# One fp32 transformer layer with eight routed experts on one core: scaled rows scattered back to token order, weights split during attention, and a plan made ahead of the experts

## What is computed

```python
mod = silu(c) @ wmod                      # six rows of 256 for each batch: sa, ca, ga, sb, cb, gb
h = layernorm(x) * (1 + ca) + sa
x = x + ga * attention(h)                 # one head of 128, keys of the whole batch
h = layernorm(x) * (1 + cb) + sb
shared = (silu(h @ sg) * (h @ su)) @ sd   # 256 -> 512 -> 256
scores, experts = top_k(sigmoid(h @ router + bias), 2);  scores /= sum(scores)
combined = sum over the two chosen e of scores[e] * (silu(h @ gate[e]) * (h @ up[e])) @ down[e]
out = x + gb * (shared + combined)
```

## Time and profile before

| | |
|---|---|
| time, median of 3 | 1787.32 us |
| the profiled execution: its own time, its span | 1788.52 us, 1786.8 us |
| PE busy | 1645.2 us (92%), 10888 instructions |
| DVE busy | 1046.3 us (59%) |
| ACT busy | 826.2 us (46%) |
| POOL busy | 497.9 us (28%) |
| moved by DMA | 134.34 MB, 75 GB/s over the span |

### The profile page before, as it was taken

One profiled execution on the slowest core, in us unless ns is written; L12 is line 12 of the kernel. 1 busy time (PEld: TensorE's weight loads), 2 busy tenths in 40 slices (PEclk: granted clock), 3 DMA queues, 4 the chain that ended last, 5 costly groups with the idle time before them and its releaser, 6 DMA issues. The chain is left out here.

```text
span 1786.8 us, 34539 instructions
## 1 busy us (share of the span) xinstructions
PE 1645.2 (92%) x10888; PEld 1492.6 (84%) x10889; DVE 1046.3 (59%) x2242; ACT 826.2 (46%) x1628; POOL 497.9 (28%) x504
## 2 busy tenths in 40 slices
PE   8899999999999959897609999999999999988997
PEld 7899999999999848797508888888888888877886
DVE  6777777777778757576533333333333333338987
ACT  5566666565655545455203333333333333335553
POOL 4423223222000030654751020111022400007775
PEclk9999999999999969999859999999999999999999
DMA  3211111111011060211252121122122111114544
GB/s 113 95 43 42 42 42 45 40 47 37 25 37 36 25 230 7 89 73 60 104 192 99 53 88 56 53 91 88 54 90 90 53 53 56 53 43 122 159 144 139
DMA packets 102463, 134.34 MB, mean 75 GB/s; under 512 B 11620, under 2 KB 89572, under 8 KB 102252
## 3 DMA queue, kind: packets, MB, share of 16 engines
q1 hardware_dynamic: 85948, 86.56, 14.8%
q0 software_dynamic: 15312, 44.58, 7.5%
q10 hardware_dynamic: 1120, 2.10, 0.3%
HBM read 79.71 MB, written 53.49 MB: 75 GB/s over the span
## 5 line engine op out<-in xcount | busy, mean ns | idle before, releaser
L794 DVE TENSOR_TENSOR e_aT_lo<-e_bank,e_aT_hi 128x512 fp32r<-128x512 f32 x136 | 94.1, 692 | 239.2 <-ACT e_aT_hi L781 239.2
L757 PE MATMUL e_bank<-e_w_hi,e_xT_hi 128*128 x544 | 225.9, 415 | 0.0
L757 PE MATMUL e_bank<-e_w_hi,e_xT_lo 128*128 x544 | 214.0, 393 | 0.0
L757 PE MATMUL e_bank<-e_w_lo,e_xT_hi 128*128 x544 | 213.3, 392 | 0.0
L800 DVE TENSOR_TENSOR e_prod<-e_silu_g,e_bank 128x512 f32<-128x512 f32 x136 | 93.6, 688 | 189.9 <-PE e_bank L757 189.9
L1394 ACT ACTIVATE e_y<-e_bank 128x256 f32<-128x256 f32 x136 | 52.2, 384 | 320.8 <-PE e_bank L33 320.8
L1565 POOL DMA_INDIRECT y<-y_rows,place_i x128 | 131.7, 1029 | 218.1 <-POOLq L1253 179.4
L608 DVE TENSOR_REDUCE bmax<-s_pair 128x1 f32<-128x512 f32 (+1 forms) x192 | 166.1, 866 | 12.1 <-PE s_pair L33 9.1
L346 ACT ACTIVATE pT_hi<-t_pair 128x512 fp32r<-128x512 f32 (+1 forms) x192 | 136.0, 749 | 78.6 <-PE t_pair L470 76.8
L627 DVE TENSOR_TENSOR pT_lo<-t_pair,pT_hi 128x512 fp32r<-128x512 f32 (+1 forms) x192 | 160.1, 862 | 17.5 <-ACT pT_hi L346 15.5
L339 ACT ACTIVATE prob<-s_pair,negmax 128x1024 f32<-128x1024 f32 x128 | 141.7, 1116 | 57.1 <-DVE negmax L620 51.2
(11 more groups left out here) (294 smaller groups left out, 4562.9 us busy)
## 6 DMA issues: line engine op xcount, KB each, us to landing
e_h<-x_rows SPq DMA_DIRECT2D x136, 128.0 KB, 2.0
y_rows<-e_y SPq DMA_DIRECT2D x136, 128.0 KB, 1.7
XS<-in_x SPq DMA_DIRECT2D x32, 256.0 KB, 2.7
XR<-in_x SPq DMA_DIRECT2D x32, 256.0 KB, 2.6
x<-XR SPq DMA_DIRECT2D x32, 256.0 KB, 2.1
out<-Z SPq DMA_DIRECT2D x16, 512.0 KB
Z<-x SPq DMA_DIRECT2D x2, 2048.0 KB, 15.6
e_w_raw<-in_gate_w POOLq DMA_DIRECT2D x7, 512.0 KB, 4.2
```

Of the source, the lines that this page charges most:

```text
L757: mm = pe.matmul(out[:, 0:I], l, w, start=(c == 0 and k == 0), stop=(c == HC - 1 and k == 2))
L794: dve.tensor_tensor(flat(aT_lo, par), a_bank[:, 0:I], flat(aT_hi, par).bitcast(F32), ALU.subtract).then_inc(f.aT_lo_done, 1)
```

## The change

- **Weights.** All 27 matrices (three shared, 24 of the experts) are split during attention: SP loads one in a row-block (`load_piece`), POOL splits it (`split_piece`), SP stores both parts to `w_parts` in DRAM (`store_piece`). Nothing is split afterwards. The shared parts are loaded once and stay (`w_shared`); each expert's six parts are one DMA of 3 MB from SP into one of two halves of `w_all`.
- **Statistics** of the new rows are joined during attention on DVE (`join_statistics`) and finished on POOL (`deviations`).
- **Shared stage.** DVE writes the normalised rows straight into a ring of four groups of four steps; ACT's copy is gone. There are eight groups. Each row in the ring and in `x_rows` is four numbers longer: token, first place, and two numbers from which either score follows. After the 32 double steps eight single steps follow with tiles 32 to 39; during these the counts are known, the pads are stored, and DVE makes the plan in three parts. All groups are sent before the stage ends.
- **Experts.** ACT issues the loads of rows. DVE copies the four numbers (`rides`) and makes destination and score (`tell`). ACT scales the output by the score, and POOL scatters it with one indirect DMA to the token's row of `y_rows`, first choices in one half and second in the other. SP only loads weights.
- **Last stage.** 24 steps. There are no gathers: SP loads chunks of four tiles from both halves of `y_rows`, six chunks ahead; POOL adds them and multiplies by the gate row; DVE adds them to `Z`.

```diff
+            def load_piece(i):
+                if i:
+                    sp.wait_ge(piece_out, 32 * i)
+                sp.dma_start(piece_raw[:], d.matrices[i]).then_inc(piece_in, 16)
+
+            def store_piece(i):
+                sp.wait_ge(piece_split, 2 * i + 2)
+                o = W * (i % 3)
+                for part, src in enumerate((piece_hi[:].bitcast(F32), piece_raw[:])):
+                    sp.dma_start(d.w_parts[i // 3, :, part, o:o + W], src).then_inc(piece_out, 16)
...
+                if 0 <= G - 2 < PIECES:
+                    store_piece(G - 2)
+                if 0 <= G - 1 < PIECES:
+                    load_piece(G - 1)
...
+            def split_piece(i):
+                pool.wait_ge(piece_in, 16 * i + 16)
+                pool.tensor_copy(piece_hi[:], piece_raw[:]).then_inc(piece_split, 1)
+                pool.wait_ge(piece_split, 2 * i + 1)
+                pool.tensor_tensor(piece_raw[:].bitcast(F32R), piece_raw[:], piece_hi[:].bitcast(F32),
+                                   ALU.subtract).then_inc(piece_split, 1)
...
+                if m >= NG + 2:
+                    split_piece(m - NG - 2)
+                for b in range(NB - 2):
+                    if m == NG * (b + 2) + 4:
+                        deviations(pool, d, b)
...
+                for b in range(NB - 1):
+                    if G == NG * (b + 1) + 2:
+                        dve.wait_ge(d.stats1_done, 2 * NG * (b + 1))
+                        join_statistics(dve, d, b)
...
+def join_statistics(dve, d, b):
...
+    tb = slice(d.TB * b, d.TB * b + d.TB)
+    mean = lambda k: d.stats1[:, tb, 3 * k + 1]
+    second = lambda k: d.stats1[:, tb, 3 * k + 2]
+    gap, both, squares = d.mean_gap[:, tb], d.mean_sum[:, tb], d.squares[:, tb]
+    dve.tensor_tensor(gap, mean(0), mean(1), ALU.subtract).then_inc(d.moments, 1)
+    dve.tensor_tensor(both, mean(0), mean(1), ALU.add).then_inc(d.moments, 1)
+    dve.tensor_tensor(squares, second(0), second(1), ALU.add).then_inc(d.moments, 1)
+    dve.wait_ge(d.moments, 5 * b + 3)
+    dve.scalar_tensor_tensor(out=gap, in0=gap, scalar=(d.row - 4) / 4.0, in1=gap,
+                             op0=ALU.mult, op1=ALU.mult).then_inc(d.moments, 1)
+    dve.wait_ge(d.moments, 5 * b + 4)
+    dve.tensor_tensor(squares, squares, gap, ALU.add).then_inc(d.moments, 1)
+
...
+def deviations(pool, d, b):
+
+    tb = slice(d.TB * b, d.TB * b + d.TB)
+    pool.wait_ge(d.moments, 5 * b + 5)
+    pool.tensor_scalar(d.mean_gap[:, tb], d.squares[:, tb], 1.0 / (d.row - 4), EPS, ALU.mult, ALU.add
+                       ).then_inc(d.rstd_done, 1)
+    pool.wait_ge(d.rstd_done, 2 * b + 1)
+    pool.tensor_tensor(d.rstd[:, tb], d.mean_gap[:, tb], d.minus_half[:], ALU.pow).then_inc(d.rstd_done, 1)
...
+def columns_of(parts, lo_at, o, n):
+
+    return lambda c: parts[:, o + n * c:o + n * c + n], lambda c: parts[:, lo_at + o + n * c:lo_at + o + n * c + n]
...
+        spare = d.w_all[:, 1, :].bitcast(F32)
+        SLOT = 2 * GS * ROW
+        in_slot = lambda ap: ap.rearrange("p (s t h) -> p s t h", s=2, t=GS)
+        h_rows = [in_slot(spare[:, SLOT * i:SLOT * i + SLOT]) for i in range(RING // 2)]
+        h_rows += [sb(f"h_rows{i}", [P, 2, GS, ROW], F32) for i in range(RING // 2)]
...
+            for k in range(3):
+                if k == 2:
+                    sp.dma_start(rows[:, :, 0:H], d.mod_d.rearrange("o (b n) -> o b n", b=NB)[:, :, 3 * H:4 * H]
+                                 .to_broadcast([P, NB, H])).then_inc(gate_loaded, 16)
+                for part in range(2):
+                    o = 3 * W * part + W * k
+                    sp.dma_start(d.w_shared[:, o:o + W].bitcast(F32), d.w_parts[0, :, part, W * k:W * k + W]
+                                 ).then_inc(w_loaded[2 + k], 16)
             for b in ORDER:
...
+            sp.wait_ge(d.s_const, d.n_tables)
+            sp.dma_start(d.x_rows[d.spare_row:d.spare_row + P * E, :].rearrange("(e p) h -> p e h", p=P),
+                         d.pad[:].unsqueeze(1).to_broadcast([P, E, ROW])).then_inc(padded, 16)
+            sp.dma_start(d.w_all[:, 0, :].bitcast(F32), d.w_parts[1].rearrange("p a n -> p (a n)")).then_inc(d.w_ready, 16)
+            sp.wait_ge(free_known, 1)
+            for e in range(E):
+                row = sp.value_load(free_i[0:1, e:e + 1], min_val=0, max_val=d.all_rows - P)
+                sp.dma_start(d.x_rows[ds(row, P), :], d.pad[:]).then_inc(padded, 16)
             for b in ORDER:
                 sp.wait_ge(x_loaded[b], 16)
+            sp.wait_ge(gate_loaded, 16)
+            sp.wait_ge(d.w_ready, 16)
...
-            def shift(m, par, b):
+            def shift(m):
                 dve.wait_ge(scaled_done, m + 1)
-                if inside(m - 2, STEPS):
-                    dve.wait_ge(f.xT_mm, m - 1)
-                    dve.wait_ge(copied, m - 1)
-                dve.tensor_tensor(h[:, par, :, :], scaled[:, par, :, :], both_halves(b, H),
+                g = m // GS
+                if m < STEPS and m % GS == 0 and g >= RING:
+                    dve.wait_ge(sent[g % RING], ONCE * (g // RING))
+                dve.tensor_tensor(rows_at(m), scaled[:, m % 2, 0:streams(m), :], both_halves(m, H),
                                   ALU.add).then_inc(f.rows_ready, 1)
...
+            def plan_ends():
+                dve.wait_ge(sent[PLAN_GROUP % RING], ONCE * (PLAN_GROUP // RING + 1))
+                op(dve.tensor_tensor(count[:], base[:, GROUPS, :], d.first_row[:, 0:E], ALU.subtract))
+                op(dve.tensor_tensor(over, count[:].unsqueeze(2).to_broadcast([P, E, d.most]),
+                                     c.limits[:].unsqueeze(1).to_broadcast([P, E, d.most]), ALU.is_gt))
+                op(dve.tensor_reduce(nblocks[:], over, AX_X, ALU.add))
+                op(dve.tensor_copy(ends[:], nblocks[:]))
+                for e in range(1, E):
+                    op(dve.tensor_tensor(ends[:, e:e + 1], ends[:, e - 1:e], nblocks[:, e:e + 1], ALU.add))
+
+            def plan_experts():
+                op(dve.memset(starts[:, 0:1], 0.0))
+                op(dve.tensor_copy(starts[:, 1:E + 1], ends[:]))
+                op(dve.scalar_tensor_tensor(out=moved[:], in0=starts[:], scalar=-float(P), in1=d.first_row[:, 0:E + 1],
+                                            op0=ALU.mult, op1=ALU.add))
+                op(dve.tensor_tensor(jump[:], moved[:, 1:E + 1], moved[:, 0:E], ALU.subtract))
+                op(dve.tensor_tensor(behind[:], c.numbers[:].unsqueeze(2).to_broadcast([P, NBLK, E]),
+                                     ends[:].unsqueeze(1).to_broadcast([P, NBLK, E]), ALU.is_ge))
+                op(dve.memset(expert_of[:, 0:2], 0.0))
+                op(dve.tensor_reduce(expert_of[:, 2:], behind[0:1, :, 0:E - 1], AX_X, ALU.add))
+                by_pair = expert_of[:].rearrange("o (i two) -> o i two", two=2)
+                digit = [by_pair[:, 0:NBLK // 2, 0], by_pair[:, 0:NBLK // 2, 1],
+                         by_pair[:, 1:NBLK // 2 + 1, 0], by_pair[:, 1:NBLK // 2 + 1, 1]]
+                so_far = digit[3]
+                for k in (2, 1, 0):
+                    op(dve.scalar_tensor_tensor(out=packed[:, k], in0=so_far, scalar=float(E), in1=digit[k],
+                                                op0=ALU.mult, op1=ALU.add))
+                    so_far = packed[:, k]
+                op(dve.tensor_copy(d.table[:, 1, 0:NBLK // 2], packed[:, 0]))
+
+            def plan_rows():
+                op(dve.tensor_tensor(behind[:], behind[:], jump[:].unsqueeze(1).to_broadcast([P, NBLK, E]), ALU.mult))
+                op(dve.tensor_reduce(moved_by[:], behind[:], AX_X, ALU.add))
+                op(dve.tensor_tensor(d.block_rows[:], c.own_rows[:], moved_by[:], ALU.add))
+                op(dve.tensor_copy(d.table[:, 0], d.block_rows[0:1]))
+                op(dve.tensor_copy(d.ends_i[:], ends[0:1]))
...
+                if n % GS == 0 and 0 < n <= STEPS:
+                    place(n // GS - 1)
+                if n % GS == GS - 1 and n < STEPS:
+                    choose(n // GS)
+                if n == STEPS:
+                    dve.tensor_copy(free_i[:], base[0:1, GROUPS, :]).then_inc(free_known, 1)
+                if n == STEPS + 2:
+                    plan_ends()
+                if n == STEPS + 3:
+                    plan_experts()
+                if n == STEPS + 4:
+                    plan_rows()
...
+            for e in range(1, E):
+                if e >= 2:
+
+                    end = sp.value_load(d.ends_i[0:1, e - 2:e - 1], min_val=1, max_val=NBLK)
+                    hold(sp, d, f.y_mm, end)
+                    sp.wait_ge(d.w_ready, 16 * e)
+                sp.dma_start(d.w_all[:, e % 2, :].bitcast(F32), d.w_parts[e + 1].rearrange("p a n -> p (a n)")
+                             ).then_inc(d.w_ready, 16)
+            sp.wait_ge(d.w_ready, 16 * E)
...
+            def scatter(m, par):
+                if inside(m - 1, NBLK):
```

(68 more changed lines are left out.)

910 lines of the change are left out of this document (361 added, 549 removed).

## The result

The changed kernel takes 1875.61 us (median of 4 runs, 1872.39 to 1877.09) against 1787.88 us for the kernel before beside it: 1.0487 of its time, 95% interval 1.0469 to 1.0505. It is slower by 88 us; 1775 was forecast. The profiled execution has a span of 1870.6 us, 83.8 more than before's 1786.8.

What follows compares the result with a forecast made beforehand. PE was taken to bound the experts at 4.84 us a block, POOL's gathers to pace the last stage. Terms -1 + 28 + 15 - 54 = -12 us from 1787.3 gave 1775 us, range 1738 to 1808.

Steps and rivals of the forecast that it cites:

- The loop: Experts: ride, ACT's load, output, low parts and product close a loop once a block, 5.05 us against 4.84; +28 us.
- Rival 2: Experts: the loop is 5.25 us or more, through register read and issue in ACT's queue; 1809 at 5.3; chance 0.16.
- Rival 4: Experts: the register read is slow on ACT, 0.454 us, so the loop is 5.23 us; 1799; chance 0.04.
- The weight loads: Experts: six weight loads of 7.7 us delay rows issued 8 us before their need, 2.5 us each; +15 us.
- rival 3: Loop 5.05 us, but each of six weight loads stalls the block 5 us and last-stage chunks come late; 1800; chance 0.10.
- The last stage: Steps of 4.68 us, POOL's sums running ahead and DVE's wide additions in idle time; 135.8 us in all, -53.7 us.
- Before the first shared product: Kernel start to first shared product: attention's additions +1 us, start of the shared stage gains 5 us; -4.
- The 31 double-step intervals: Shared stage: a ring of four groups removes 31.5 us of waits, seven group ends cost 28.7; -3 us.
- the single steps with the plan and the way into the experts: Last double step to first expert product: 51 us for eight single steps and plan, 25.3 into the experts; 76.3 us.
- 11.5 - 6 = 5.7: Single steps: the plan's 27 DVE operations take 11.5 us in three places, 2 us hidden in each; 5.7 left.
- POOL's 27 splits: Attention: loading, splitting and storing 27 pieces falls in POOL's idle time; put at 0, bounds 0 and +8 us.
- Rival 1: Experts: the loop does not bind, PE keeps 4.84 us a block, weight loads cost some 8 us; 1740; chance 0.28.

Runs made afterwards that it cites:

- weights_in_six: Changed kernel with each of the last six experts' 3 MB weight loads cut into six loads, one released a block; experts 710.7 us, 46.1 less; whole time 1906.0 us.
- all_four: Changed kernel with ride and score ahead of DVE's product, weight loads in six spaced pieces, POOL's last-stage operations 256 columns wide; 1738.73 us, 0.9711 of the kernel before.
- the first four kernels: Changed kernel with one edit each, sharing a chip: load later, ride earlier, weight loads cut, POOL operations shortened; 1900.1, 1864.1, 1906.0, 1922.3 us.

## Why the prediction was wrong

Three prices were wrong, all three too low; 1875.6 lies above the whole range (1738 to 1808) and above every rival.

**The loop: right in kind, mis-sized.** "Sum 5.05 us against 4.84" is 5.02 in the trace, and its terms (eight are listed, not ten) hold within 0.1 us each: the load, for one, is 1.24 instead of 1.32. But I compared only this loop with PE's pace, and that step failed: the same chain also closes over two blocks with a whole PE step in it, and that one takes 5.28 a block, 5.25 in the mean of the 129 blocks without a stall: +55 us (135 x 0.41) instead of +28. Two cyclic paths shared the slow piece, and I had summed only the shorter. Rival 2 (5.25 or more) was the case that came, by this cause and not by its own, the register read and the issue in ACT's queue. Rival 4 is out, since the read takes 0.284 us on ACT (the row is in the last section). The Trainium skill, "DMA: Bandwidth & Descriptors", section "Latency and other measured facts", has a floor of about 600 ns for it; this trace does not agree, and the measurement decides.

**The weight loads: +48 instead of +15.** "A load is issued 8 us before its transposed copy is needed" is the step that failed: it is 5 us (1042.08 to 1047.0, when PE was through with the products and had nothing but these rows to turn). The 8 is that of the kernel before, where SP issues it: the last load of the stage goes out at 1581.6 there and is turned at 1589.6, in the changed kernel at 1679.8 and 1684.7, since the load now waits for the ride. And I had priced the wait alone (5.8 us), not the half clock behind it (the rest of 8.2). This is the first half of rival 3, at 3.2 us a load more than it had. weights_in_six gives 46 of the 48 back.

**The last stage: -11 instead of -54, the largest miss.** "DVE's 16 wide additions fall in its idle time", and POOL's sums beside it at no cost: each POOL operation of some 2.6 us held up what DVE had to do with two operands in SBUF. The price of POOL beside DVE, put at nothing, is the step that failed. The step is 148.4 / 23 = 6.45 us, not 4.68. Cutting the operations gives 25.6 of the 40.8 us back. Some 4 us of the 40.8 are not POOL's: 4.68 was read behind a late step, while undisturbed ones take 4.85 in the kernel before (its steps 2 to 10) and 4.88 in the changed one (the six intervals before its last), 23 x 0.17 to 0.20. The stage's other parts were right: 19.3 us to its first product (18.1 foretold), 10.4 from the last one to the end (10.1).

**What held.** Before the first shared product -4.0 (-4); the first gate product is at 643.6 (near 642.5 foretold). The 31 double-step intervals -7.3 (-3), the single steps with the plan and the way into the experts 73.7 us (76.3; its "11.5 - 6 = 5.7" is 5.5, a slip of 0.2). Of attention the windows up to 625 us of the kernel before and of the changed one show that POOL's 27 splits cost PE nothing:

```profile
0.00:625.00 625.00, 610.34 (x4440) 568.74 (x4441) 471.92 (x930) 371.77 (x677) 134.22 (x186) 1.00 0.15 48
```

```profile
0.00:625.00 625.00, 610.04 (x4440) 568.71 (x4441) 477.43 (x943) 371.69 (x678) 235.32 (x245) 1.00 0.35 115
```

The terms add up: the forecast's -12, and +27 (loop), +33 (weights), +42 (last stage), -7 (the rest) make +83; the spans differ by 83.8. Rival 1's gain, "the loop does not bind", is real once the loop is cut: all_four has 4.85 us a block and 1738.7 us.

What stays open: why the first four kernels have a longer shared stage at a lower clock on their chip (of the kernel before there is no trace there, only its 1917.5 us and a mean clock of 0.93 where it is 0.965 elsewhere), and what of the last stage's remaining 15 us over 4.68 a step, less the 4 above, is POOL's (with short operations `Z<-l_gy,Z` is still at 0.87 us in the mean).

## What to carry to other kernels

When an engine takes over a wait, list every closed path through it, those over two steps and through the bounding engine as well, and divide each by its steps; the slowest mean is the pace. Intervals that alternate, as 5.02 and 5.54 do here, are a sign of a path over two steps. A large transfer issued just ahead of a small one on another queue can hold it back for its whole length, here some 8 us, and the clock lost behind the stall cost another 2.4 on 5.8 us of waiting: cut the transfer into pieces and release one a block, since pieces issued all at once brought a third of the gain. Here work moved to POOL cost nothing beside DVE operations that read PSUM and held up those with both operands in SBUF: keep POOL's operations short there, or leave DVE the slack.
